# Attention with an expert layer on one core: value products in whole and half groups behind bursts of 3, 3 and 2 score pairs, and score maxima taken in three pieces

## What is computed

```
xn  = layernorm(x)                                  # x: 2 x 2048 x 256
q, k, v = split(xn @ w_qkv.T), 16 heads of 16; q, k = rope(q), rope(k)
attn = softmax(q @ k.T / 4)                         # per batch and head, 2048 x 2048
s   = (attn @ v) @ w_out.T
e   = argmax(xn @ gate_w.T)                         # one of 8 experts per token
g   = silu(square(relu(xn @ wg[e])) * (xn @ wu[e]) @ wd[e])
out = x + s * g
```

## Time and profile before

| | us |
|---|---|
| median of 3 runs | 1527.42 (1527.12 to 1528.42) |
| span of the profiled execution | 1524.1 |
| PE busy | 1494.0 (98%) |
| DVE busy | 1383.3 (91%) |
| ACT busy | 1229.4 (81%) |
| granted TensorE clock | full speed in all 40 slices of the span |

### The profile page before, as it was taken

One profiled execution on the slowest core, in us unless ns is written; L12 is line 12 of the kernel. 1 busy time (PEld: TensorE's weight loads), 2 busy tenths in 40 slices (PEclk: granted clock), 3 DMA queues, 4 the chain that ended last, 5 costly groups with the idle time before them and its releaser, 6 DMA issues.

```text
span 1524.1 us, 35757 instructions
## 1 busy us (share of the span) xinstructions
PE 1494.0 (98%) x13325; PEld 630.1 (41%) x13325; DVE 1383.3 (91%) x1483; ACT 1229.4 (81%) x2381; POOL 161.7 (11%) x221
## 2 busy tenths in 40 slices
PE   7999999999999999999999999999999999999998
PEld 5655433333584333333333333333333333333336
DVE  6689999999747999999999999999999999999906
ACT  4553588888768888888888888888888888888891
POOL 5332423100002211000010000000000000000110
PEclk9999999999999999999999999999999999999999
DMA  5873244345253464333333342222332423333303
GB/s 189 282 198 123 62 85 86 59 74 93 61 174 80 78 130 71 47 47 47 47 47 47 47 102 44 42 42 38 46 45 41 97 37 47 47 47 47 68 13 115
DMA packets 77753, 117.72 MB, mean 77 GB/s; under 512 B 28946, under 2 KB 64146, under 8 KB 70674
## 3 DMA queue, kind: packets, MB, share of 16 engines
q1 hardware_dynamic: 71650, 103.72, 34.9%
q0 software_dynamic: 3072, 8.39, 2.2%
q10 hardware_dynamic: 2896, 3.62, 0.7%
HBM read 75.05 MB, written 39.71 MB: 75 GB/s over the span
## 4 chain that ended last, share of the span: by engine, by line
PE 91%; ACT 5%; issue 1%; DVE 1%; DMA 1%; SPq 0%; POOL 0%; ACTq 0%; POOLq 0%
PE ps L1221 41%; PE ps L1234 36%; ACT arena L643 3%; PE ps L1137 3%; PE ps L1396 2%; PE ps L1138 1%; PE ps L1349 1%; PE ps L1333 1%; ACT arena L608 1%; PE ps L1170 1%; PE ps L1162 1%; PE ps L1209 1%; PE ps L1149 1%; PE ps L1300 1%; PE ps L1342 0%
## 5 line engine op out<-in xcount | busy, mean ns | idle before, releaser
L643 ACT ACTIVATE arena<-ps 128x512 f32<-128x512 f32 x2048 | 1108.7, 599 | 156.7 <-PE ps L1221 76.7
L792 DVE TENSOR_REDUCE arena<-ps 128x1 f32<-128x1024 f32 x992 | 1204.6, 1220 | 23.6 <-PE ps L1209 17.6
L1221 PE MATMUL ps<-qs,ks 50*128 50x512 f32 x2048 | 734.8, 444 | 0.3 <-ACT arena L647 0.3
L1209 PE MATMUL ps<-ks,qs 48*128 48x512 f32 x1984 | 722.5, 444 | 0.0
L1234 PE MATMUL ps<-arena 128*32 128x256 f32 x8192 | 651.0, 391 | 11.8 <-ACT arena L608 7.3
L1221 PEld LDWEIGHTS ps<-qs,ks 50*128 50x128 f32 x2048 | 297.4, 185 | 415.2 <-issue 407.3
L1234 PEld LDWEIGHTS ps<-arena 128*32 128x32 f32 x8192 | 165.0, 108 | 382.5 <-issue 380.6
L1209 PEld LDWEIGHTS ps<-ks,qs 48*128 48x128 f32 x1984 | 292.3, 185 | 3.7 <-issue 2.5
L1062 POOL COPY arena<-v_sb 128x256 f32 (+1 forms) x32 | 13.2, 416 | 931.8 <-ACT arena L608 921.2
L1137 PE MATMUL ps<-arena 128*128 128x512 f32 x128 | 69.2, 623 | 0.7 <-ACT arena L555 0.7
L564 ACT COPY arena<-ps 128x512 f32<-128x512 f32 x32 | 18.7, 585 | 53.5 <-PE ps L1138 53.4
(11 more groups left out here) (112 smaller groups left out, 569.4 us busy)
## 6 DMA issues: line engine op xcount, KB each, us to landing
qs<-parts_d SPq DMA_DIRECT2D x186, 128.0 KB, 4.5
ks<-parts_d SPq DMA_DIRECT2D x186, 128.0 KB, 5.0
parts_d<-arena SPq DMA_DIRECT2D x64, 256.0 KB, 2.6
xs_d<-arena SPq DMA_DIRECT2D x13, 384.0 KB, 3.7
arena<-xs_d SPq DMA_DIRECT2D x13, 384.0 KB, 3.8
ys_d<-arena SPq DMA_DIRECT2D x13, 384.0 KB, 2.8
onum_d<-arena SPq DMA_DIRECT2D x124, 32.0 KB
arena<-onum_d SPq DMA_DIRECT2D x3, 1024.0 KB
```

The costliest lines, as they stand in the source:

```text
L643: nc.scalar.activation(prob[kb % 2][:, c * W:(c + 1) * W], ps[:, bank, :], ACT.Exp, scale=SCALE).then_inc(exp_done[bank], 1)
L792: nc.vector.tensor_reduce(most[head_slot][:, tile, u:u + 1], ps[:, AB + 2 * u:AB + 2 + 2 * u, :], AX.XY, ALU.max).then_inc(a_reduced[u], 1)
L1209: ins = nc.tensor.matmul(ps[:, AB + c, :], qs[head_slot][ABASE:ABASE + KR, tile * P:(tile + 1) * P].bitcast(F32R), ks[head_slot][ABASE:ABA ...
L1221: nc.tensor.matmul(ps[:, bank, :], ks[s][at:at + KS, kb * P:(kb + 1) * P].bitcast(F32R), qs[s][at:at + KS, c * W:(c + 1) * W].bitcast(F32R ...
```

## The change

- **Values.** TensorE's order has a round of two steps, eight score pairs (`ROUND`). Behind pair 0 stands a whole value group of 512 columns, behind pair 3 and behind pair 5 a half one. Between value groups this gives bursts of 3, 2 and, across the round's border, 3 score pairs. The value groups are those of the two steps before the round that is being scored (`weigh_behind`): the whole one belongs to the first of them, the two halves to the second.
- **Probabilities.** There are four `prob` buffers, taken by step modulo 4. Two of them lie in `x_sb`, the on-chip copy of x rows 0 to 15 of 32. SyncE loads these rows again (`x_back`) once head 30 is weighed, and VectorE waits for that ahead of the output stage. The last head uses two buffers.
- **Maxima.** The reductions of an A step are three: piece 0 (512), piece 1 (512), pieces 2 and 3 (1024), each with its pair of semaphores.
- **Around it.** `sums_out` stands behind the second exponential of the next head's step 1 (in the last head, its third). The inversion of the sums is at step 5. The place in a pair of heads at which the rotation over three banks skips one (`BENDS`) is 25 for 28. The rotation starts anew with bank 0 at each pair of heads, before and now.

```diff
@@ constants
+    GROUPS = ((0, 1), (1, 2), (2, 4))
+    GROUP_OF = (0, 1, 2, 2)
+    ROUND = 2 * 4
         prob = [cut([L]) for _ in range(2)]
+        prob += [x_sb[:, i * KB // 2:(i + 1) * KB // 2, :].rearrange("p t d -> p (t d)") for i in range(2)]
-        BENDS = (28,)
+        BENDS = (25,)
+        def prob_of(pi, s, kb):
+            return prob[kb % (2 if last_head(pi, s) else len(prob))]
@@ sync
                     store_sums(n, s, pi)
+                    if known and n == NH - 2:
+                        for i in range(2):
+                            sp.wait_ge(pv_done[i], past((NH - 1) * NB2))
+                        sp.dma_start(x_sb[:, 0:KB, :], x_v[:, 0:KB, :]).then_inc(x_back, 16)
@@ scalar, exps
-                    act.wait_ge(pv_done[kb % 2], past(pi * KB + (s * NB2 + kb // 2)))
+                    slots = 2 if last_head(pi, s) and kb >= 2 else len(prob)
+                    if not (isinstance(pi, int) and pi * 2 * KB + s * KB + kb < slots):
+                        act.wait_ge(pv_done[kb % 2], past(pi * KB + (s * NB2 + kb // 2 + 1 - slots // 2)))
-                        if kb == 0 and c == QT - 1 and not first:
+                        if kb == 1 and c == (2 if last_head(pi, s) else 1) and not first:
                             sums_out(1 - s, pi - 1 + s)
@@ vector, reduce
+                lo, hi = GROUPS[u]
                 dve.wait_ge(a_scored[u], t + (1 - KB))
-                nc.vector.tensor_reduce(most[head_slot][:, tile, u:u + 1], ps[:, AB + 2 * u:AB + 2 + 2 * u, :], AX.XY,
-                                        ALU.max).then_inc(a_reduced[u], 1)
+                if hi - lo == 1:
+                    nc.vector.tensor_reduce(most[head_slot][:, tile, u:u + 1], ps[:, AB + lo, :], AX.X,
+                                            ALU.max).then_inc(a_reduced[u], 1)
+                else:
+                    nc.vector.tensor_reduce(most[head_slot][:, tile, u:u + 1], ps[:, AB + lo:AB + hi, :], AX.XY,
+                                            ALU.max).then_inc(a_reduced[u], 1)
-                if kb == 4:
+                if kb == 5:
                     invert(1 - s, pi + s)
@@ vector, ahead of the output stage
                         dve.wait_ge(gate_ready, 16 * NT)
+                        dve.wait_ge(x_back, 16)
@@ tensor
-            def weigh_values(pi, s, kb, half):
+            def weigh_values(n, lo, hi):
+            def weigh_behind(p, first):
+                place, step = p % ROUND, first + (p - first * QT) // ROUND * 2 - 2
+                if p < first * QT + ROUND:
+                    return
+                if place == 0:
+                    weigh_values(step, 0, W)
+                elif place == 3:
+                    weigh_values(step + 1, 0, W // 2)
+                elif place == 5:
+                    weigh_values(step + 1, W // 2, W)
@@ tensor, pair: behind each score pair
-                            if last_head(pi, s):
+                            if last_head(b_pi, b_slot) or last_head(pi, s):
+                                if s == 1 and kb == 0 and c == QT - 2:
+                                    weigh_values(g - 1, 0, W)
                                 if c == QT - 1:
-                                    weigh_values(pi, s, kb, 0)
-                                    weigh_values(pi, s, kb, 1)
-                            elif c % 2:
-                                weigh_values(pi, s, kb, c // 2)
-                                if held_back and c == 1:
+                                    weigh_values(g - (s == 0), 0, W)
+                            elif held_back:
+                                if c == 0:
+                                    weigh_values(g - 1, 0, W)
+                                elif c == QT - 1:
                                     open_experts()
+                                    weigh_values(g, 0, W)
+                            else:
+                                weigh_behind((g + 1) * QT + c, first)
```

More of the change, by code:

```diff
@@ L162, in layer_kernel @@
         at[0] = HEADS_AT
-        most = [cut([KB, 2]) for _ in range(2)]
+        most = [cut([KB, len(GROUPS)]) for _ in range(2)]
+        most_early = most[0].rearrange("p t c -> p (t c)")[:, 0:2 * KB].rearrange("p (t u) -> p t u", u=2)
         best_m = cut([KB])
@@ L258, in layer_kernel @@
         e_reduced = sem("e_reduced")
-        a_scored = [sem(f"a_scored{i}") for i in range(2)]
-        a_reduced = [sem(f"a_reduced{i}") for i in range(2)]
+        a_scored = [sem(f"a_scored{i}") for i in range(len(GROUPS))]
+        a_reduced = [sem(f"a_reduced{i}") for i in range(len(GROUPS))]
         mrow_ready = sem("mrow_ready")
@@ L276, in layer_kernel @@
         last_stored = sem("last_stored")
+        x_back = sem("x_back")
         sums_spread = sem("sums_spread")
@@ L642, in exps @@
                         act.wait_ge(scored[bank], b_before(pi, s, kb, c) + 1)
-                        nc.scalar.activation(prob[kb % 2][:, c * W:(c + 1) * W], ps[:, bank, :], ACT.Exp,
+                        nc.scalar.activation(prob_of(pi, s, kb)[:, c * W:(c + 1) * W], ps[:, bank, :], ACT.Exp,
                                              scale=SCALE).then_inc(exp_done[bank], 1)
@@ L751, in reduce_early @@
                 dve.wait_ge(e_scored, n + 1)
-                nc.vector.tensor_reduce(most[0][:, t, u:u + 1], ps[:, 6:8, :], AX.XY, ALU.max).then_inc(e_reduced, 1)
+                nc.vector.tensor_reduce(most_early[:, t, u:u + 1], ps[:, 6:8, :], AX.XY, ALU.max).then_inc(e_reduced, 1)
             early = [0]
@@ L800, in cut_maxima @@
                     else:
-                        for u in range(2):
+                        for u in range(len(GROUPS)):
                             dve.wait_ge(a_reduced[u], past(head * KB))
-                    link(nc.vector.tensor_reduce(best_m, most[head_slot], AX.X, ALU.max), wait=False)
+                    parts = most_early if isinstance(head, int) and head == 0 else most[head_slot]
+                    link(nc.vector.tensor_reduce(best_m, parts, AX.X, ALU.max), wait=False)
                 else:
@@ L871, in step @@
                     experts_of_tiles(pi * 2 + s - 1)
-                if kb == 4:
+                if kb == 5:
                     invert(1 - s, pi + s)
-                for u in range(2):
+                for u in range(len(GROUPS)):
                     if not last_pair or (s == 0 and ahead < KB):
                         reduce(g + AHEAD, (s + 1 + ahead // KB) % 2, ahead % KB, u)
-                    k = 2 * (ahead - KB) + u + 1
-                    if 0 <= k < CUTS and coming:
+                    k = 2 * (ahead - KB) + u // 2 + 1
+                    if u != 1 and 0 <= k < CUTS and coming:
                         cut_maxima(k, pi * 2 + (s + 1), 1 - s, s, (pi + 1) * 64)
@@ L1204, in score_a @@
             def score_a(t, head_slot, tile, c):
-                u, half = divmod(c, 2)
-                if half == 0:
+                u = GROUP_OF[c]
+                if c == GROUPS[u][0]:
                     pe.wait_ge(a_reduced[u], past(t - KB))
@@ L1210, in score_a @@
                                        ks[head_slot][ABASE:ABASE + KR, c * W:(c + 1) * W].bitcast(F32R), start=True, stop=True)
-                if half:
+                if c == GROUPS[u][1] - 1:
                     ins.then_inc(a_scored[u], 1)
@@ L1277, in pair @@
                             pe.wait_ge(shift_loaded[b_slot], (pi + 1 + s) * 64 + 64 * last_head(b_pi, b_slot))
+                        first = FB * 2 * KB if pi >= FB else 0
                         for c in range(QT):
```

19 lines of the change are left out of this document (10 added, 9 removed).

## The result

The changed kernel takes 1484.39 us (median of 4 runs, 1482.99 to 1487.58) for 1527.55 before (median of 4): a ratio of 0.9724, with a 95% interval of 0.9711 to 0.9738. The forecast was 1475 in a range of 1463 to 1497. The sign and the mechanism are right. The gain is 43 us where 53 was forecast.

What follows compares the result with a forecast made beforehand. TensorE was taken to bind before, VectorE after (4.73 us a round). A pair of heads at 76.0 for 79.48 gave -53.5, the ends +0.4: span 1471.0, plus 3.3 as measured time, said as 1475; range 1463 to 1497.

Steps and rivals of the forecast that it cites:

- TensorE's round: TensorE's work over two steps, eight score pairs and three value groups: 4.59 us, for 4.94 before.
- third pair: Third score pair of a burst on TensorE: 0.235 us, upper end 0.335, taken from one product ahead of head 0.
- VectorE's round: VectorE's four short and two long reductions, 4.66 us, with small operations 4.73; more than TensorE needs, so VectorE binds.
- The "slower" rival: Three reductions cost VectorE more than its slack, break-even 4.90 us a round; 1557, 1560 or 1602 us; chance 0.06.
- That the order lets VectorE run through: Within a round VectorE never waits for scores, by margins of 0.07 to 0.4 us.
- the bad place: Start of a pair of heads: rotation begins with bank 0 though bank 1 is oldest; pair 0 waits 0.6 us.
- about half: Share of TensorE's 0.6 us wait at a pair of heads' start that VectorE feels: 0.3 us a pair.
- my own timeline: Start times in one round, from pair 0 at 0, with when scores reach VectorE and when its reductions end.
- the four small operations: VectorE's operations for the maxima and the inversion: 0.11 us each, 0.56 a head, 0.07 a round.
- two steps without values: Behind the experts two steps run without value groups, at VectorE's or ScalarE's pace: -0.6 us.
- The ends: Places outside the steady steps: -0.9, +0.5, -0.6 and +1.4 us, reload of x 0; together +0.4.
- The rival of a smaller gain: Third pair costs 0.335 us (1492), or a reduction's fixed part is 0.075 (1491); 1484 to 1494 us; chance 0.22.

Runs made afterwards that it cites:

- seamless rotation: Changed kernel with the bank rotation skipping at places 25 and 41 of a pair of heads, instead of at 25 and the border: 1475.23 us, ratio 0.9672.

## Why the prediction was right, and by how much it missed

**TensorE's round: right in every term.** Whole group 0.99 for 1.00, third pair 0.23 for 0.235, the rest as in the rows. The third pair was taken from a single product without a partner ahead of head 0; that it would hold for pairs was an assumption, and it does. Of the Trainium skill's rule in "TensorE: Matmul & The Clock Gate", section "The mechanism", by which a load runs beside matmuls only in another row group, I had worked out 0.335 for the third pair: the trace has 0.23, so the measurement decides against it here.

**VectorE's round: right.** 0.595 for 0.60 and 1.13 for 1.13. That the bound moves to VectorE is shown by the added copy, which costs 43 us in the regular heads of the changed kernel and about 1 us in those of the kernel before. The "slower" rival fell with it: its break-even was 0.04 more per instruction. The 120 cycles of "VectorE: DVE Perf Modes", section "The TRN2 errata", in the Trainium skill would have made 0.66 of a short reduction; this trace shows 0.595.

**That the order lets VectorE run through: right inside a head.** Reductions follow without a gap.

**Mis-sized: the pair's border.** I had found the bad place and its wait on TensorE (0.6; it is 0.94 - 0.23 = 0.71), and then let VectorE feel "about half", 0.3. It feels 0.61. The step that failed is the one from TensorE's wait to VectorE's: between the late pair 0 and pair 1 lies a whole value group, so that only VectorE's margin before the second short reduction can cover it. By my own timeline this margin is 0.17 (free at 1.96, scores ready at 1.79), so that a wait of 0.6 should have been priced at 0.43, and the measured 0.71 at 0.54. "About half" had no working behind it. The seamless rotation took 8 to 9 us away for a forecast of 0.61 x 15.3 = 9.3 from the trace.

**Missing: VectorE's wait for itself, 0.22 a head.** I priced the four small operations by what follows them, and not by what they wait for. It was there in the kernel before too (three reductions end at 808.49 + 3.69 = 812.18, and L803 of the earlier trace rows starts at 812.28), covered by slack. Moving the operation took 5.5 us away (0.21 x 30.6 = 6.4).

**The sum.** Per pair of heads: border +0.31, L824's wait +0.44, the reductions 0.16 cheaper than rounded, and some starts that follow a small operation 0.1 earlier: +0.46 in all, 76.46 for 76.0. Over 15.3 pairs that is 7 of the 12 us by which the span missed (1483.3 for 1471.0). The rest is in places that the forecast had priced at steady pace. By the first score of each head, the six heads ahead of the experts gained 7.0 where 9.9 were forecast, and the stretch behind them 34.7 for 43.4. Ahead of the experts 1.4 of this are the three pairs' borders and waits. Another 1.4 fits the five routing operations of VectorE in the heads 1 to 3 (0.44, 0.43, 0.19, 0.19 and 0.16 long in the kernel before), which slack had hidden and which now count. Behind the experts the first head takes 39.7 for a steady 38.2, where I had expected two steps without values to gain 0.6. The granted clock (third number from the end) accounts for the 1.5. The first two rows are of the changed kernel, the third of the changed kernel with the memset:

```profile
460.00:465.00 5.00, 5.00 (x24) 1.80 (x27) 1.40 (x3) 3.77 (x9) 1.36 (x2) 0.75 1.00 164
465.00:470.00 5.00, 5.00 (x42) 1.76 (x42) 4.54 (x6) 3.79 (x8) 0.00 (x0) 0.91 0.49 57
...
460.00:465.00 5.00, 5.00 (x29) 1.72 (x28) 2.25 (x5) 4.46 (x10) 1.67 (x2) 1.00 0.87 149
```

For part of these 10 us TensorE is granted 1.2 GHz in this execution, though its records fill the time since 455. With the memset and in the seamless rotation the clock stays full there, and the same head takes 38.35 and 38.18. So this 1.5 belongs to the clock in the profiled execution and not to the price of the change; what lowered the clock is not shown. Of the 0.6 that I had expected to gain, those two runs show little or nothing either.

And TensorE once stops for 1.2 with nothing that the profile shows to wait for, ahead of the tenth head:

```profile
572.88 1.22 issue
```

The seamless rotation has a stop at the same head, and there the profile puts it down to SyncE's transfer of the row maxima:

```profile
571.27 0.47 PE L1243 MATMUL ps<-qs,ks 50*128 50x512 f32 x1 [0.70 <-DMA qs<-arena]
```

A late transfer is thus the likely cause of the 1.2 too, but no run tested it. The ends came out as forecast: +0.3 from the last A product to the output stage, for +0.5, and the reload of x was hidden. An estimate that adds the pieces: 7 + 1.4 + 1.5 + 0.6 + 1.2 = 11.7 of the 12.3.

**The rival of a smaller gain** would have been at 1484 to 1494, and the time is there, but not by its causes, both of which the trace denies (0.23 for the third pair, 1.13 and 0.595 for the reductions). A number inside a rival's range doesn't confirm the rival.

## What to carry to other kernels

Engine records that touch each other don't show a full engine: the cost of an instruction is the distance to the next start in a stretch where nothing is waited for, and the test of a bound is to add work to that engine whose own distance is seen in the trace. Switching between two ways of tiling the array costs each time, so group the work of one kind as far as the banks allow, and cut the consumer's pieces so that the first bank of a burst comes free early. When a change spends another engine's slack, list what that engine's slack has been hiding (waits for itself, borders, odd jobs), because each of these now counts in full.

## What the runs showed of the hardware

**A memset between two reductions is nearly free** on VectorE: 128 x 56 costs 0.01 to 0.02 us, a copy of the same size 0.094.

**A copy on VectorE is held up by a long GpSimd operation.** In the kernel before with the added copy, first VectorE, then GpSimd:

```profile
790.58 2.55 DVE L872 COPY scratch<-ident 128x56 f32<-128x56 f32 x1
```

```profile
788.52 4.56 POOL L1071 TENSOR_TENSOR arena<-arena 128x2048 f32<-128x2048 f32 x1
```

The copy, 0.18 elsewhere, lasts 2.55, until 793.13, and GpSimd's product of 128 x 2048 ends at 793.08. It is the same at the next such product, 329 us later, and in the changed kernel with the copy (3.97 us). The reductions, which read PSUM, pass beside the same product without loss: in the kernels without the copy there is no such gap. The Trainium skill says as much in "SBUF — State Buffer", section "SBUF: two separate sides": the port pair that both engines share is locked for a whole instruction, and the loser is blocked; this trace agrees for an fp32 copy, which ends within 0.1 us of GpSimd's product.

**Such a stall can cost more than itself.** In head 14 of the kernel before with the copy TensorE starts 2.0 us late, 1.49 of them idle, and is then granted half its clock, 1.2 GHz, for some 20 us. Stretches of that trace (busy time of PE, PEld, DVE, ACT, POOL, then the granted clock):

```profile
800.00:805.00 5.00, 5.00 (x34) 1.69 (x28) 3.39 (x5) 2.32 (x5) 0.00 (x0) 0.50 0.02 2
...
820.00:825.00 5.00, 5.00 (x56) 1.82 (x48) 4.99 (x7) 4.42 (x9) 0.00 (x0) 1.00 0.00 0
```

TensorE is called busy throughout in either, but does 34 instructions for 56. That makes head 14 of that run 10.7 us too long. The other stall of the same length, in head 22, again with 1.49 idle, was not followed by a lower clock and cost 2.0. In the changed kernel with the copy TensorE stood idle for 2.72 at both products, and both times a shorter stretch at half clock followed (granted 0.60 and 0.72 on average over the 10 us from 793, 0.66 over the 5 us from 1118); these heads were 5.8 and 4.7 too long. So what a stall costs isn't told by its length alone.
